# Fused cross-attention and mixture-of-experts kernel: moving the preparation of three batches within the opening

## The reference

```python
def _L0_xattn_ref(x, latents, mask, ...):     # x: context, latents: layernorm of the tokens
    xn = layernorm(x, ln_x_g, ln_x_b)
    ln = layernorm(latents, ln_l_g, ln_l_b)
    q = (ln @ Wq).reshape(b, m, h, d).transpose(0, 2, 1, 3)
    kv = jnp.concatenate([xn @ Wkv, ln @ Wkv], axis=1)
    ...
    qn = rmsnorm(q, qn_g) * scale
    kn = rmsnorm(k, kn_g)
    sim = jnp.einsum('bhid,bhjd->bhij', qn, kn)
    ...
    out = jnp.einsum('bhij,bhjd->bhid', attn, v)
    return out @ Wout + bout
...
x = x + _L0_xattn_ref(ctx_1024, _layernorm(x, axis=-1), ...)
x = x + _L0_ffn_ref(_layernorm(x, axis=-1), ...)
```

## Time and profile before

| | |
|---|---|
| median of 3 runs | 2509.13 us (2508.64 to 2511.17) |
| profiled execution, its own time | 2505.31 us |
| span of its instructions | 2503.8 us |
| PE busy | 2408.4 us, 96% of the span |
| DVE, ACT, POOL busy | 1749.3, 1689.1, 1212.2 us |
| mean granted clock of PE | 0.988 |

### The profile page before, as it was taken

How to read it: one execution, slowest core, us unless ns; L and a number is a source line. 1 busy time by engine, 2 the same in 40 slices (tenths; PEclk the granted TensorE clock), 3 DMA queues, 4 the chain that set the end, 5 groups by cost and what they waited for, 6 DMA issues and landing times. The chain is left out here.

```text
span 2503.8 us, 53762 instructions
## 1 busy us (share of the span) xinstructions
PE 2408.4 (96%) x19926; PEld 1997.1 (80%) x19926; DVE 1749.3 (70%) x2452; ACT 1689.1 (67%) x2286; POOL 1212.2 (48%) x783
## 2 busy tenths in 40 slices
PE   4899999999999999999999999988989999999997
PEld 3677777777777777777777777658989999999997
DVE  7666766676667666766676667777875567777775
ACT  2688888888888888888888888872333345444443
POOL 5444434443445344534453445425515537677766
PEclk9899999999999999999999999998999999999999
DMA  6423332323333323233333232247804279999996
GB/s 199 148 84 115 100 98 86 124 92 100 94 115 100 101 85 123 91 100 94 115 99 101 86 123 90 68 125 167 200 10 144 92 243 320 317 327 317 319 326 166
DMA packets 231532, 363.25 MB, mean 145 GB/s; under 512 B 59559, under 2 KB 139739, under 8 KB 227400
## 3 DMA queue, kind: packets, MB, share of 16 engines
q1 hardware_dynamic: 204694, 301.66, 39.2%
q0 software_dynamic: 25696, 58.82, 8.1%
q10 hardware_dynamic: 978, 0.34, 0.1%
HBM read 280.90 MB, written 79.85 MB: 144 GB/s over the span
## 5 line engine op out<-in xcount | busy, mean ns | idle before, releaser
L734 DVE TENSOR_TENSOR pr_lo<-ps_s,pr_hi 128x1024 fp32r<-128x1024 f32 x420 | 513.0, 1221 | 297.2 <-ACT ps_s L844 297.2
L843 ACT ACTIVATE pr_hi<-ps_s 128x1024 fp32r<-128x1024 f32 x512 | 527.4, 1030 | 133.5 <-PE ps_s L991 110.1
L476 POOL TENSOR_TENSOR rs<-ss,minus_half 128x16 f32<-128x16 f32 (+1 forms) x96 | 226.8, 2362 | 555.4 <-DVE ss L709 555.4
L1700 ACT ACTIVATE ht<-f_ps_h,b 128x256 f32<-128x256 f32 x440 | 184.6, 471 | 338.8 <-PE f_ps_h L1632 338.8
L1027 PE MATMUL ps_o<-pr_hi,vA 64*65 64x512 f32 x1780 | 378.2, 391 | 2.5 <-DVE pr_lo L734 2.5
L1027 PE MATMUL ps_o<-pr_lo,vA 64*65 64x512 f32 x1780 | 377.2, 390 | 0.0
L1027 PE MATMUL ps_o<-pr_hi,vC 64*65 64x512 f32 x1780 | 376.5, 390 | 0.0
L844 ACT ACTIVATE ps_s<-ps_s 128x1024 f32<-128x1024 f32 x360 | 370.9, 1030 | 0.0
L1632 PE MATMUL f_ps_h<-xT_hi,w 128*128 128x256 f32 x1760 | 353.5, 284 | 3.3 <-DVE xT_lo L1734 2.3
L957 PE MATMUL ps_m<-w_sb,lnT_sb 64*128 64x384 f32 (+1 forms) x3072 | 326.0, 335 | 11.7 <-POOL w_sb L532 4.8
L1645 PE MATMUL f_ps_y<-w,h_hi 128*128 128x256 f32 x1760 | 325.6, 283 | 0.0
(11 more groups left out here) (220 smaller groups left out, 4698.3 us busy)
## 6 DMA issues: line engine op xcount, KB each, us to landing
w<-w1S_dram SPq DMA_DIRECT2D x160, 512.0 KB, 6.2
lnT_sb<-lnT_dram SPq DMA_DIRECT2D x31, 2304.0 KB, 8.9
w2raw<-in_L_ffn_Wproj SPq DMA_DIRECT2D x78, 512.0 KB, 7.0
w1S_dram<-cut POOLq DMA_DIRECT2D x36, 512.0 KB, 3.0
rec<-rden_dram SPq DMA_DIRECT2D x63, 256.0 KB, 3.7
routed_dram<-empty POOLq DMA_DIRECT2D x28, 387.0 KB, 3.5
xt<-routed_dram SPq DMA_DIRECT2D x39, 258.0 KB, 6.7
w_raw<-in_L_xattn_Wkv SPq DMA_DIRECT2D x66, 128.0 KB, 2.9
```

Source lines behind the costliest of these rows:

```text
L476: g.tensor_tensor(rs[:, 0:sums], ss[:, 0:sums], minus_half[:, 0:sums], ALU.pow).then_inc(s_pool, 1)
L734: v.tensor_tensor(pr_lo[:, ring(w, d), :], full_of(w, d), pr_hi[:, ring(w, d), :].bitcast(F32), ALU.subtract).then_inc(s_lo, 1)
L843: act.activation(pr_hi[:, ring(w, d), :], ps_s[:, d % 2, :], ACT.Exp, bias=bias)
L1700: ins = act.activation(ht[:, p, i, :], ps_h[:, p % 2, i, :], ACT.Gelu_apprx_tanh, bias=b1[:, slot, p, i:i + 1])
```

## The change

Nothing is added or removed in the computation; instructions change places in the two windows that attend nothing.

- Window (-1, 0): the six steps of batch 1 stood at units 8 to 13, between the tiles of the first pair. Now PE and ACT do them at d = 17, behind all nine tiles, and DVE at d = 13; `centre(2)` moves from d = 12 to d = 17, behind the second `squares`. `deviation(2)` on POOL moves behind the first product of squares, `deviation(3)` behind `lower_w`.
- Window (-1, 1): the steps of batch 2 move from units 1 to 6 to units 5 to 10 (`SECOND`), those of batch 3 from units 8 to 13 to units 12 to 17 (`THIRD`). `statistics(3)` moves from d = 0 to d = 2, `centre(3)` from d = 5 to d = 10.

```diff
--- before.py
+++ after.py
@@ -85,6 +85,7 @@
 JOBS = TURNS + KT
 PREP = [(c, g) for g in range(2) for c in range(C)] + [(c, None) for c in range(C)]
 PREPS = len(PREP)
+SECOND, THIRD = 5, 12
 NORMS = ((0, 4), (4, 8), (8, 9))
 GROUPS = len(NORMS)
 MOST_TILES = 4
@@ -472,6 +473,8 @@
                 if w.turn and k != 1:
                     pool.wait_ge(s_job, turn_job(w, TURNS - 1 if k else AHEAD - 1))
                 g.tensor_tensor(sq[:, 0:n_, j0 * DH:], qk, qk, ALU.mult).then_inc(s_sq, 1)
+                if isinstance(w.v, int) and w.v == -1 and w.s == 0 and k == 0:
+                    deviation(2)
                 pool.wait_ge(s_ss, w.n(2 * GROUPS, 4 * GROUPS + 2 * k + 2))
                 g.tensor_tensor(rs[:, 0:sums], ss[:, 0:sums], minus_half[:, 0:sums], ALU.pow).then_inc(s_pool, 1)
                 pool.wait_ge(s_pool, w.n(GROUPS, 2 * GROUPS + k + 2))
@@ -515,14 +518,12 @@
                     last = isinstance(w.v, int) and w.v == 2 * E - 1
                     load1(fc_s[0:1] if last else fc_v[bass.ds(w.v + 1, 1)])
                 opening = isinstance(w.v, int) and w.v == -1
-                if opening and w.s == 0:
-                    deviation(2)
                 if w.proj:
                     for k in range(GROUPS):
                         normalise(w, k)
-                        if opening and w.s == 0 and k == 1:
-                            deviation(3)
                     lower_w(w.other, w.n(1, 4))
+                if opening and w.s == 0:
+                    deviation(3)
                 if opening and w.s == 1:
                     pool.wait_ge(p_split, 2 * PREPS * B)
                     load1(fc_v[0:1])
@@ -630,21 +631,22 @@
                     if d == 0:
                         centre(1)
                         statistics(2)
-                    if 8 <= d < 8 + PREPS:
-                        split(1, d - 8)
-                    if d == 12:
+                    if d == 13:
+                        for j in range(PREPS):
+                            split(1, j)
+                    if d == UNITS - 1:
                         centre(2)
                 else:
-                    if 1 <= d < 1 + PREPS:
-                        split(2, d - 1)
+                    if d == 2:
+                        statistics(3)
                     if d == 3:
                         squares(w, 2 - GROUPS)
-                    if d == 0:
-                        statistics(3)
-                    if d == 5:
+                    if SECOND <= d < SECOND + PREPS:
+                        split(2, d - SECOND)
+                    if d == SECOND + PREPS - 1:
                         centre(3)
-                    if 8 <= d < 8 + PREPS:
-                        split(3, d - 8)
+                    if THIRD <= d < THIRD + PREPS:
+                        split(3, d - THIRD)
 
             def maximum(w, h):
 
@@ -805,13 +807,14 @@
             def opening(w, d):
 
                 if w.s == 0:
-                    if 8 <= d < 8 + PREPS:
-                        scaled(1, d - 8)
+                    if d == UNITS - 1:
+                        for j in range(PREPS):
+                            scaled(1, j)
                 else:
-                    if 1 <= d < 1 + PREPS:
-                        scaled(2, d - 1)
-                    if 8 <= d < 8 + PREPS:
-                        scaled(3, d - 8)
+                    if SECOND <= d < SECOND + PREPS:
+                        scaled(2, d - SECOND)
+                    if THIRD <= d < THIRD + PREPS:
+                        scaled(3, d - THIRD)
 
             def upper(d):
 
@@ -892,13 +895,14 @@
             def opening(w, d):
 
                 if w.s == 0:
-                    if 8 <= d < 8 + PREPS:
-                        prep(1, d - 8)
+                    if d == UNITS - 1:
+                        for j in range(PREPS):
+                            prep(1, j)
                 else:
-                    if 1 <= d < 1 + PREPS:
-                        prep(2, d - 1)
-                    if 8 <= d < 8 + PREPS:
-                        prep(3, d - 8)
+                    if SECOND <= d < SECOND + PREPS:
+                        prep(2, d - SECOND)
+                    if THIRD <= d < THIRD + PREPS:
+                        prep(3, d - THIRD)
 
             for j in range(PREPS):
                 prep(0, j)
```

## The result

| | before | after |
|---|---|---|
| median | 2508.61 us (2504.31 to 2512.48, 20 runs) | 2514.36 us (2511.87 to 2516.70, 20 runs) |
| profiled execution, its own time | 2505.31 | 2513.42 |
| span | 2503.8 | 2511.9 |
| granted clock | 0.988 | 0.985 |

The ratio is 1.0022 with a 95% interval of 1.0016 to 1.0028: 5.75 us slower, where I forecast 3.5 slower. The sign and most of the mechanism are as forecast, and 2514.36 lies in the range. But the difference is over the 5.0 us that I set as the bound of "no change" (a ratio of 1.0020, which lies inside the interval), so it came out on the slow side, to which I gave 0.18.

The account below looks back on a forecast made before the run. PE is full from window (0, 0)'s tile 0, so only that start moves: lead 2.6 at the second pair, -0.2 at tile 5, first exponential 4.1 late, taken as 3.5. 2509.1 + 3.5 = 2512.6 us, range 2507 to 2517.

Parts of the forecast that it names:

- the slow side: Whole kernel: slower than before by more than 0.2% (5.0 us); chance 0.18.
- PE's lead in the first window: Window (-1, 0): tiles end at 43.8 instead of 48.1, 4.3 us of lead, of which 0.5 remains at the second sum of squares.
- The first tile at 67.0: Second pair's first tile, released by `lower_w`: lead of 2.3 to 2.9 us, taken as 2.6.
- Tiles 2 and 3 at the low clock: Window (-1, 1): behind eight transposes of batch 2 (1.97), these tiles take 4.7 and end at 78.3; lead 1.5.
- rival 1: From the first pair's end PE's clock comes back earlier and casts miss POOL's products: -0.3, 2508.8 us; chance 0.22.
- `k_lo` at 86.0, lead gone: Ahead of tile 5, window (-1, 1): PE waits for `k_lo` behind DVE's splits and `centre(3)`; tile 5 at 86.3, lead -0.2.
- rival 4: Clock stays low through tiles 5 to 8 of window (-1, 1): some 2.6 more, 2515.2 us; chance 0.08.
- The first exponential 4.1 late, taken as 3.5: Behind window (-1, 1)'s tiles, batch 3's last steps put it at 97.9 instead of 93.75; 3.2 without the last collision.
- the rounding "against me": At the first exponential: allowance for rounding in many small sums, with 3.5 taken instead of 4.1.
- Behind it nothing is absorbed.: From the first exponential to window (0, 0)'s tile 0 and the end: the delay goes through unchanged.
- rival 3: Reload of `lnT_sb` late for window (0, 0), landing 110.1 to 114.1: at worst 1.7 late, 2514.3 to 2514.9 us; chance 0.10.
- The port.: DVE and POOL share an exclusive port lock: the power would hold back `centre(2)` some 3 us ahead of `lower_w`; 2 in 100.

Follow-up runs that it names:

- e3: Kernel after plus idle PE transposes that nothing reads, at five places of window (-1, 1) (22, 16, 24, 5, 10); 2513.74 us, ratio 1.0024 to before.
- e11: Kernel after plus idle PE turns only at the end of window (-1, 1) (6, 6, 12 in units 15, 16, 17); 2514.10 us, ratio 1.0024 to before.
- e7: Kernel after with `centre(3)` at d = 5, behind split(2, 0), instead of d = 10; 2509.63 us, ratio 1.0002 to before.
- e5: Kernel after with POOL's squares of tiles 0 to 3 in window (-1, 1) waiting for `centre(3)`; 2513.88 us, ratio 1.0021 to before.
- e6: Kernel after with `THIRD` = 11 instead of 12, each step of batch 3 one unit earlier; 2514.39 us, ratio 1.0021 to before.
- e10: e9 plus idle PE turns in its waits of window (-1, 1) (22, 8, 4, 6, 6); 2505.60 us, ratio 0.9987 to before.
- e12: e10 with the load of `lnT_sb` for window (0, 0) issued ahead of batch 3's stores instead of behind them; 2501.81 us, ratio 0.9970 to before.
- e8: First window as before, second as in the kernel after but `THIRD` = 11 and `centre(3)` at d = 5; 2505.22 us, ratio 0.9986 to before.
- e2: Kernel after with the first window as before, so only the second window's half of the change; 2509.83 us, ratio 1.0003 to before.
- e4: Kernel before plus idle PE transposes in window (-1, 1), 22 behind unit 3 and 16 behind unit 5; 2506.37 us, ratio 0.9991 to before.
- e9: e8 with the next pair's weights load issued ahead of batch 2's stores on SP's queue instead of behind; 2504.95 us, ratio 0.9982 to before.

## Why the prediction was right or wrong

- **PE's lead in the first window.** Forecast: tiles end at 43.8, second sum of squares at 53.2. Measured 45.8 and 53.67. The first of the two was off because I took the copies of tiles 2 and 3 from the trace before, where these tiles took 3.08; in the profile after they took 4.83 (at 32.35), the pace of the low clock, and their copies end at 38.1, not 35.7. Before:

```profile
31.68 3.08 PE L957 MATMUL ps_m<-w_sb,lnT_sb 64*128 64x384 f32 x24 [0.58 <-ACT raw L788]
```

The change doesn't make this difference: in e3 and e11, whose program is that of the kernel after up to there, the same tiles took 3.08 and 3.07, tile 8 ended at 43.6 and 43.4, and the second sum of squares stood at 52.8 and 52.9. So the forecast of 43.8 fits those executions. (That it was the clock is read from the pace. In the profile after, the column of the granted clock says 1.00 there; in e7, where these tiles took 5.01, it says 0.50.) The second number was nearly right even so; the first cast lost only 0.34 to POOL's squares (0.76 against 0.42), because it came 1.4 into them.
- **The first tile at 67.0.** Mis-sized by 1.4, for two reasons that lie side by side. `lower_w` took 2.97, not 2.03, beside DVE's `vC` (65.24, 1.35; the last point below); and the load of `lnT_sb`, which I took for hidden, landed at 68.25. It was issued 3.7 later than before (56.95 against 53.24), since the stores of batch 1 stand ahead of it on SP's queue and these wait for the splits that the change moved. Before:

```profile
53.24 1.05 SPq L296 DMA_DIRECT2D lnT_sb<-lnT_dram  x1
```

I counted this wait for window (0, 0) only. In e3, e5, e6 and e7 the profile names this load as what ends PE's wait.
- **Tiles 2 and 3 at the low clock.** Wrong, in the good direction: 2.69 instead of 4.7, a part of rival 1. They end at 77.3, not 78.3, in spite of the later start: this error hides the one before it, and that is luck.
- **`k_lo` at 86.0, lead gone.** Right in its mechanism and nearly in its size (85.03). What I missed is that PE's wait there, 4.5, costs the clock: tiles 5 and 6 took 3.66, not 2.7. That is a part of rival 4. Tiles 7 and 8 end at 93.3 (forecast 92.9).
- **The first exponential 4.1 late, taken as 3.5.** It is 4.7 late (98.41; my sum had 97.9), and the tail took 5.1 (5.0 in the sum). The collision of the last large cast with POOL's squares came (1.28), and the rounding "against me" that I allowed for took away what was right; this was a choice, not a row.
- **"Behind it nothing is absorbed."** True, but something is added, and this is the step that failed (as a term that was put at nothing): 16.0 from the exponential to tile 0 instead of 14.5. Two things lie there. `q_lo` is ready at 113.69, 15.28 behind the exponential instead of 14.46: the low clock under scores and turned parts, 0.8 (e10 and e12 show up to 1.5). And PE, done with its scores at 113.87, waits 0.53 more for `lnT_sb`: rival 3, with its stores at 98.93 (forecast 98.8) and its landing at 114.3 (forecast 110.1 to 114.1). I gave this rival 0.10. That its price (2514.3 to 2514.9) is the time that was measured is luck: the load cost 0.5 at tile 0, not the 1.7 that I counted, and the rest came from the clock and the earlier terms.
- **The port.** The rule of the Trainium skill, SBUF — State Buffer, section "Who interferes with whom", an exclusive lock for a whole instruction, fits two subtractions here that read two tensors in SBUF each, whichever of them starts first. In the kernel after `vC` started 0.04 ahead of `lower_w`, ran its 1.35, and `lower_w` took 2.97. The timeline of e8, where POOL was first:

```profile
63.22 1.81 POOL L533 TENSOR_TENSOR w_sb<-w_raw,w_sb 128x768 fp32r<-128x768 f32 x1
63.84 2.40 DVE L689 TENSOR_TENSOR vC<-raw,vA 128x1152 fp32r<-128x1152 f32 x1
```

Here `lower_w` ran its 1.81 and `vC` took 2.40, so that the tiles could start. For the power the rule doesn't hold as it stands: in the trace after, too, `centre(2)` took 2.66 beside a power of 2.99, and a cast (at 86.85) and a subtraction (at 87.31) took their 0.43 and 0.69 beside another. But the power is not free of it. Started 0.16 behind DVE's subtraction of 1024 columns (91.79, 1.22), it took 3.81 instead of 2.90 in e10, and as long in the same place before the change:

```profile
91.95 3.81 POOL L478 TENSOR_TENSOR rs<-ss,minus_half 128x16 f32<-128x16 f32 x1 [1.90 <-DVE ss L711]
```

In sum: 4.7 + 0.8 + 0.5 makes the 6.1 at tile 0 within rounding, against 5.75 by the medians. Left out were two losses of the same kind, waits of PE with the low clock behind them, and the late load, in both windows. Why the clock's part differs from execution to execution (tiles 2 and 3 of the first window, e2's profile, e10 against e12) stays open, as does how much of e12's gain beyond 1.7 is its edit.

## What to carry to other kernels

A load that stands behind a store in one engine's program is issued no sooner than the store, so a step that is moved later moves every load queued behind its result; read each load's issue plus its time to landing against the start of its reader, in each window, even where the profile names another releaser or only "issue". Price a long wait of PE (3.3 us and more here) with the tiles behind it at the low clock, not by its own length alone, and take that price as uncertain from one execution to the next. And put a step that has no reader soon into the time in which its engine stands idle: one line, `centre(3)` five units sooner, gave back 4.7 of the 5.75, with some 2.7 of uncertainty.

## What was not expected of the hardware

- 38 turns of a 128x128 tile that nothing reads, in PE's waits, brought the next pair of tiles from 4.63 to 2.70 at an unchanged start (e4); the same 38 left it at 4.03 in e3, and 30 of them gave 4.16 in e10 and 2.72 in e12.
- The load of `lnT_sb` (2304 KB) for window (0, 0) took 10.7 to 12.7 from issue to landing in all of these profiles, with stores queued ahead of it (after, 12.2) or behind it (e12, 11.1), so that its landing moved with its issue.
- Two executions of the same kernel can differ by 3.9 us (e2's profile and its median), and in the profiles the same tiles ran at the pace of either level of the clock: tiles 2 and 3 of the first window took 3.07 to 3.10 in seven of them (before, e2, e3, e4, e8, e9, e11) and 4.57 to 5.01 in the other seven.
- POOL's power on 128x16 took 3.81 instead of 2.90 when DVE's subtraction of two tensors had started 0.16 ahead of it (e10), and a cast and a subtraction of DVE that started later than a power kept their own time.
